# One GpSimd product over four states in place of two over two, in the scan stage of a convolution and Mamba kernel

## The reference, cut to what matters

```python
xc = silu(causal_conv4(xi) + conv_b)                     # per inner channel
dt, Bm, Cm = split(xc @ xproj_w.T, [4, 16, 16])
dt = softplus(dt @ dt_w.T + dt_b)
def step(h, inp):                                        # along the sequence
    dA = exp(dt_t[:, :, None] * A)
    h = dA * h + dt_t[:, :, None] * B_t[:, None, :] * u_t[:, :, None]
    y = einsum('bes,bs->be', h, C_t)                     # sum over the 16 states
    return h, y
y = (ys + xc * D) * silu(z)
out = y @ out_w.T
```

## Time and profile before

| | before |
|---|---|
| median of 3 runs | 3948.51 us |
| the profiled execution | 3952.92 us, span 3951.1 us |
| VectorE busy | 3750.3 us (95%) |
| TensorE matmul busy | 3655.9 us (93%) |
| GpSimd busy | 3278.0 us (83%) |
| ScalarE busy | 2937.1 us (74%) |
| DMA queue of the spread chunks | 78.3% of 16 engines |

### The profile page before, as it was taken

How to read it: one execution, slowest core, us unless ns; L and a number is a source line. 1 busy time by engine, 2 the same in 40 slices (tenths; PEclk the granted TensorE clock), 3 DMA queues, 4 the chain that set the end, 5 groups by cost and what they waited for, 6 DMA issues and landing times. The chain is left out here.

```text
span 3951.1 us, 34661 instructions
## 1 busy us (share of the span) xinstructions
PE 3655.9 (93%) x8780; PEld 1520.5 (38%) x8780; DVE 3750.3 (95%) x3409; ACT 2937.1 (74%) x4422; POOL 3278.0 (83%) x1542
## 2 busy tenths in 40 slices
PE   7999999899999999999999999999999999999998
PEld 3444444333333333333333333333333333333333
DVE  7778787999999999999999999999999999999998
ACT  3454554788777788888888878888888888887785
POOL 2221222899999999999999999999999999999998
PEclk9999999999999999999999999999999999999999
DMA  4142324888889888988889988899888898998886
GB/s 113 33 130 57 108 73 151 322 341 341 340 344 353 344 342 348 349 346 338 347 347 344 352 352 345 343 351 347 347 339 346 346 346 347 352 351 340 343 345 254
DMA packets 203159, 1181.08 MB, mean 299 GB/s; under 512 B 30960, under 2 KB 31760, under 8 KB 68816
## 3 DMA queue, kind: packets, MB, share of 16 engines
q1 hardware_dynamic: 200128, 1177.64, 78.3%
q10 hardware_dynamic: 2832, 1.23, 0.1%
HBM read 1144.03 MB, written 34.73 MB: 298 GB/s over the span
## 5 line engine op out<-in xcount | busy, mean ns | idle before, releaser
L1547 POOL TENSOR_TENSOR read<-state,bc_all 128x1024 f32<-128x1024 f32 x1024 | 2399.4, 2360 | 127.6 <-DVE state L1611 97.7
L1611 DVE TENSOR_TENSOR_SCAN state<-decays,p_drive 128x1024 f32<-128x1024 f32 x1024 | 2297.8, 2274 | 35.2 <-ACT p_drive L1446 12.2
L1316 PE MATMUL p_y<-read,ident 128*128 128x512 f32 x4096 | 1920.5, 602 | 12.8 <-POOL read L1547 12.8
L1438 ACT ACTIVATE decays<-dt,wa 128x496 f32<-128x496 f32 x2048 | 1337.1, 703 | 122.1 <-DVE state L1611 119.7
L1316 PEld LDWEIGHTS p_y<-read,ident 128*128 128x128 f32 x4096 | 766.2, 191 | 987.6 <-issue 841.8
L1598 DVE TENSOR_TENSOR p_drive<-bc_all,p_dtx 128x1024 f32<-128x1024 f32 x768 | 906.3, 1210 | 0.0
L1564 POOL TENSOR_TENSOR pool_drive<-dtx,bc_all 128x1024 f32<-128x1024 f32 x256 | 602.4, 2353 | 4.4 <-DMA bc_all<-bc_scratch 4.2
L766 POOL TENSOR_TENSOR pad<-map_all,xc 128x512 f32<-128x512 f32 x96 | 139.5, 1483 | 519.1 <-DMA map_all<-map_scratch 455.3
L1446 ACT COPY p_drive<-pool_drive 128x1024 f32<-128x1024 f32 x256 | 260.8, 1019 | 271.5 <-DVE state L1611 271.5
L1312 PE MATMUL p_y<-xconv,d_diag 128*128 128x512 f32 x256 | 145.1, 649 | 204.2 <-DVE gated L1621 204.2
L556 PE MATMUL p_conv<-pad,wm 128*128 128x512 f32 x576 | 267.6, 600 | 1.2 <-issue 0.8
(11 more groups left out here) (162 smaller groups left out, 3215.7 us busy)
## 6 DMA issues: line engine op xcount, KB each, us to landing
bc_all<-bc_scratch SPq DMA_DIRECT2D x1024, 1024.0 KB, 7.2
map_all<-map_scratch SPq DMA_DIRECT2D x48, 512.0 KB, 5.7
norm_rows<-xn SPq DMA_DIRECT2D x32, 280.0 KB, 5.6
norm_in<-norm_rows SPq DMA_DIRECT2D x64, 140.0 KB, 8.1
norm_in<-norm_rows SPq DMA_DIRECT2D x64, 139.8 KB, 8.3
fresh<-in_x SPq DMA_DIRECT2D x32, 256.0 KB, 6.6
x<-in_x SPq DMA_DIRECT2D x32, 256.0 KB, 3.5
mid_x<-x SPq DMA_DIRECT2D x32, 256.0 KB, 6.5
```

The source lines that it names most:

```text
L1316: nc.tensor.matmul(p_y[:], ident[:], read[:, s % DEEP, :], start=False, stop=(s == N - 1)).then_inc(y_added, 1)
L1438: nc.scalar.activation(decays[:, s % DEEP, :].rearrange("p (q t) -> p q t", t=SIDE)[:, :, 1:], dt[b][:, :, 1:], ACT.Exp, scale=wa[m][:, s: ...
L1547: nc.gpsimd.tensor_tensor(read[:, s % DEEP:s % DEEP + 2, :], state[:, s % DEEP:s % DEEP + 2, :], bc_all[s // CHUNK][:, :, 1, :], ALU.mult) ...
L1611: nc.vector.tensor_tensor_scan(state[:, at:at + 2, :].rearrange("p s n -> p (s n)"), decays[:, at:at + 2, :].rearrange("p s n -> p (s n)") ...
```

## The change

Chunks 0 and 1, 2 and 3, 4 and 5 now lie next to each other in one tile `bc_four{n}` of [128, 4 states, 2, 512]; chunks 6 and 7 keep tiles of their own. `read_states` takes the number of states. For states 0 to 3, 4 to 7 and 8 to 11 GpSimd issues one product of [128 x 2048] in slots 3, 7 and 11, which raises `read_done` by two; states 12 and 13 and states 14 and 15 are multiplied as before, in slots 13 and 15.

```diff
@@ -1058,12 +1058,14 @@
-    bc_all = [sb(f"bc_all{k}", [128, CHUNK, 2, PIX]) for k in range(CHUNKS - 1)]
+    bc_four = [sb(f"bc_four{n}", [128, 2 * CHUNK, 2, PIX]) for n in range(3)]
+    bc_all = [bc_four[k // 2][:, CHUNK * (k % 2):CHUNK * (k % 2) + CHUNK] for k in range(CHUNKS - 2)]
+    bc_all.append(sb(f"bc_all{CHUNKS - 2}", [128, CHUNK, 2, PIX])[:])
...
-    bc_all.append(sb(f"bc_all{CHUNKS - 1}", [128, CHUNK, 2, PIX]))
+    bc_all.append(sb(f"bc_all{CHUNKS - 1}", [128, CHUNK, 2, PIX])[:])
@@ -1161,7 +1163,7 @@
-        sp.dma_start(bc_all[k][:].rearrange("p s j n -> p (s j n)"),
+        sp.dma_start(bc_all[k].rearrange("p s j n -> p (s j n)"),
@@ -1537,15 +1539,18 @@
-        def read_states(u, b, s):
-            pool.wait_ge(bc_loaded[s // CHUNK], 16 * u + 16)
-
-            ge(pool, y_added, N * u + s + 2 - DEEP)
-            pool.wait_ge(scan_done, PAIRS * u + s // 2 + 1)
-            if u == 0 and s == DEEP - 2:
+        def read_states(u, b, s, states):
+
+            for k in range(s // CHUNK, (s + states) // CHUNK):
+                pool.wait_ge(bc_loaded[k], 16 * u + 16)
+
+            ge(pool, y_added, N * u + s + states - DEEP)
+            pool.wait_ge(scan_done, PAIRS * u + (s + states) // 2)
+            if u == 0 and s == DEEP - 4:
                 pool.wait_ge(s1["stored"][0], STORED)
-            nc.gpsimd.tensor_tensor(read[:, s % DEEP:s % DEEP + 2, :], state[:, s % DEEP:s % DEEP + 2, :],
-                                    bc_all[s // CHUNK][:, :, 1, :], ALU.mult).then_inc(read_done, 1)
+            spread = bc_four[s // 4][:, :, 1, :] if states == 4 else bc_all[s // CHUNK][:, :, 1, :]
+            nc.gpsimd.tensor_tensor(read[:, s % DEEP:s % DEEP + states, :], state[:, s % DEEP:s % DEEP + states, :],
+                                    spread, ALU.mult).then_inc(read_done, states // 2)
@@ -1570,8 +1575,10 @@
-                if s % 2:
-                    read_states(u, b, s - 1)
+                if s % 4 == 3 and s < N - 4:
+                    read_states(u, b, s - 3, 4)
+                elif s % 2 and s > N - 4:
+                    read_states(u, b, s - 1, 2)
```

## The result

The changed kernel takes 4636.66 us (median of four runs, 4636.43 to 4640.92) against 3950.23 us for the kernel before on the same occasions: a ratio of 1.1735, 95% interval 1.1715 to 1.1755. It is slower by 686 us, where 523 were forecast, and it lies above the range, which ended at 4570. The profiled execution took 4636.87 us; (4636.87 - 3952.92)/126 is 5.43 us a unit in place of 4.15. The mean granted clock of TensorE has gone from 0.99 to 0.90.

What follows compares the result with a forecast made beforehand. VectorE bounds the kernel before at 25.18 us a unit; the late state 4 delays the convolution and the next scan 0 to 29.33. 126 x 4.15 = 523 us on 3952.9 gives 4476, median 4472 us, range 4410 to 4570.

Steps and rivals of the forecast that it cites:

- Length and start of the products: On GpSimd, 2048-element products take 4.52 us, running t = 6.90 to 11.42 and 13.17 to 17.69 after scan 0 starts.
- The path from the convolution to scan 0: From TensorE's convolution through ScalarE's drive move to VectorE's next scan 0: 10.64 us when nothing else decides.
- Number of units: Each unit delays the next while a unit u+2 remains to project: 126 times 4.15 us, 523 us.
- The step that failed: On TensorE, states 0 to 3 are added in time, so it waits for state 4 by about t = 16.
- The rival of the clock: TensorE idles 2.99 us a unit, its clock halves, costing 11.2 us a unit, about 5350 us; chance 0.04.
- "All hidden" of product 8 to 11: On GpSimd, the product of states 8 to 11 runs from 20.05 to 24.57 and adds no time.
- the first loop: Scan 3, product 4 to 7, state 4's addition, convolution, drive move, next scan 0: 4.15 us more each unit.
- The chunk for pair 4: Chunk 4's DMA lands 2.7 us into the next unit, hidden with 1.8 to spare; late-landing rival 4570 us, chance 0.09.

Runs made afterwards that it cites:

- e11: The changed kernel with four zero-weight products in TensorE's idle time, three behind the skip term and one behind the addition of state 3: 4477.64 us.
- e4: The changed kernel with TensorE's projection out of the last unit moved ahead of the skip term: 4593.28 us.
- e3: The kernel before with only states 8 to 11 merged into one product, all other states in pairs: 4256.28 us.
- e6: The changed kernel with TensorE's projection out ahead of the skip term and the first two projections of unit u+2 ahead of state 4: 4156.85 us.
- e8: The changed kernel with TensorE's projection out, skip term and first two projections of unit u+2 all ahead of the addition of state 0: 4219.27 us.
- e10: The kernel before, all products in pairs, with TensorE's projection out, skip term and first projections of unit u+2 ahead of state 0: 3963.16 us.
- e5: The changed kernel with TensorE's first two projections of unit u+2 ahead of state 4, those to B, C and dt one slot earlier: 4493.91 us.
- e2: The kernel before with only states 4 to 7 merged into one product, all other states in pairs: 4692.93 us.

## Why the prediction was wrong

The direction, the bound, and the place of the new wait were right; the time lay 165 us too low and outside the range.

- *Length and start of the products:* right. 4517 ns for 4524, and both products within 0.01 us of their forecast places.
- *The path from the convolution to scan 0:* right, 10.70 for 10.64, and the wait is where it was put, for the moved drive.
- *Number of units:* right. The changed kernel, e11 and e4 each show 126 such waits of VectorE.
- *The step that failed* is "TensorE itself is ready in time ... it stands waiting for state 4 by about t = 16". The prediction read 3.67 us for the additions of states 0 to 2 and the projection out from a row at full clock, so that state 3 would be begun at 11.42 + 0.04 + 3.67 = 15.13. With the clock at 0.50 they took 2038.72 - 2032.07 = 6.65, and state 3 was begun at t = 18.12. From there to the convolution are 1.82 us, so at full clock it could have started at 16.95, and the wait for state 4 until 18.69 was a cover of 1.74. The slow work used up that cover and 1.25 us more. e11, with the clock held, gives 4477.64 and so shows that this was all but 6 us of what was missing: the other terms of the sum were the right ones for the unit at full clock.
- *The rival of the clock* named the mechanism and the gap (2.99 us forecast, 2.98 measured), and failed twice. Its chance, 0.04, rested on a single gap of 2.88 us that did no harm; e4 shows gaps of one length, 2.56 and 2.57 us, going either way. And its price, 5350 us, assumed the low clock over all of TensorE's work in the path, while the clock came back after some 6 us of work, all of it ahead of the convolution. The right case lay between that rival and the forecast, where I had nothing.
- *"All hidden" of product 8 to 11:* right for the full change and wrong as a statement on that merge. e3 prices it at 305 us, and e6 and e8 show it take over as soon as the first loop is shorter.
- *The chunk for pair 4:* hidden, as forecast; it landed so that the drive started 2.89 into the unit for 2.7 in the working.
- *The two rules on record.* The Trainium skill (Perfetto Trace Analysis, Optimizing Scalar/DVE Operations) says that smaller pieces may help where ScalarE or VectorE is not saturated but leaves others idle. This case agrees for GpSimd: it was busy 83% of the span before the change, and the larger pieces cost 686 us. The Trainium skill (TensorE: Matmul & The Clock Gate, Part 1) has an idle array put back to half rate until it has been busy again. The clock rows agree (0.50 behind the gap, 1.00 again from 2038 us); the forecast had used this for a rival's chance only and not for the sum.

## What to carry to other kernels

When an edit makes a producer's results come in larger portions, look at the in-order consumer behind it: what stands behind the addition that now waits pays the delay, not the addition, and the merge is cheap or ruinous by the order of that stream (741 us against 11 for the same merge). Where the forecast gives TensorE a new idle gap of some microseconds in each period, price the work right behind the gap at the lower clock as well and see whether the cover counted on survives it. A part found "hidden" is hidden under the loop that is there; list it as the next one before shortening that loop.

## What the runs showed of the hardware that was not expected

- The length of one gap doesn't tell whether TensorE's clock falls. In the full change it fell behind 2.98 us; in e4 it fell behind 2.56 us in one unit and held behind 2.57 in the next, and behind 1.92 us it fell in 12 of the 34 units with that gap; in e10 it fell behind 2.23, and before the change it held behind 2.88.
- How much work then runs at 0.50 differs too: 5.49 us for six instructions in the full change and 4.4 to 4.5 in a third of e5's units behind the same gap, but 2.07 us for two and a part of the convolution in e2, behind a gap of 4.16.
- Products with zero weights kept the granted clock at 1.00 in e11 and made the kernel 159 us faster with 512 more of them in it.
